# Attention values divided for all tiles at once, between two stages of a graph network kernel

## The reference

```
xm = x @ W_n2m;  e = edge_attr @ W_edge;  ee = e @ W_e
q, k, v = (xm @ W_q + b_q, xm @ W_k + b_k, xm @ W_v + b_v)   as (n, H=4, C=16)
alpha = sum(q[dst] * (k[src] + ee), -1) / sqrt(C)            one per edge and head
alpha = softmax of alpha over the edges with the same dst    = ex / den[dst]
out   = segment_sum((v[src] + ee) * alpha, dst)              (n, 64)
x_r   = xm @ W_skip + b_skip
beta  = sigmoid([out, x_r, out - x_r] @ W_beta)
x     = layernorm(x + (beta * x_r + (1 - beta) * out) @ W_m2n)
x     = layernorm(x + relu(x @ w1 + segment_sum((x @ w2)[src] * ew, dst) + b))
```

## Time and profile before

| | us |
|---|---|
| median of 3 timed executions | 1562.85 (1562.12 to 1571.67) |
| span of the one profiled execution, first to last instruction | 1705.3 |
| own time of that execution | not given beside its span |
| VectorE busy in it | 1346.5 (79%) |
| TensorE busy | 1245.0 (73%) |
| ScalarE busy | 1225.0 (72%) |
| GpSimd busy | 1042.2 (61%) |

### The profile page before, as it was taken

One profiled execution on the slowest core, in us unless ns is written; L12 is line 12 of the kernel. 1 busy time (PEld: TensorE's weight loads), 2 busy tenths in 40 slices (PEclk: granted clock), 3 DMA queues, 4 the chain that ended last, 5 costly groups with the idle time before them and its releaser, 6 DMA issues.

```text
span 1705.3 us, 34722 instructions
## 1 busy us (share of the span) xinstructions
PE 1245.0 (73%) x9184; PEld 1095.8 (64%) x9184; DVE 1346.5 (79%) x5156; ACT 1225.0 (72%) x4231; POOL 1042.2 (61%) x1182
## 2 busy tenths in 40 slices
PE   1888888888888882288877876788888876665661
PEld 1877777777777772177766766666666675554551
DVE  2777898889999998888877876799999984654653
ACT  0899999999999995077787876899999962222221
POOL 2666666555566660055555656888888846666665
PEclk9999999999999996599999997999999997787876
DMA  6899999999999996734444445899999942222221
GB/s 189 269 306 302 305 305 304 303 302 301 305 301 305 308 300 233 240 117 152 154 144 140 156 141 168 270 289 292 293 289 294 292 143 77 79 82 74 86 77 38
DMA packets 210148, 372.00 MB, mean 218 GB/s; under 512 B 36740, under 2 KB 67821, under 8 KB 208935
## 3 DMA queue, kind: packets, MB, share of 16 engines
q1 hardware_dynamic: 120822, 200.48, 37.2%
q10 hardware_dynamic: 57771, 108.12, 17.3%
q0 software_dynamic: 31360, 61.17, 13.2%
HBM read 231.39 MB, written 161.37 MB: 230 GB/s over the span
## 4 chain that ended last, share of the span: by engine, by line
ACT 36%; DVE 29%; issue 11%; another core or an unknown queue 9%; PE 9%; DMA 1%; POOL 1%; SPq 1%; DVEq 1%; ACTq 0%; POOLq 0%
ACT hout L728 10%; ACT scan_buf L728 10%; DVE stats L992 7%; DVE hpre L1238 6%; ACT big L756 4%; ACT em L688 3%; DVE big L1228 3%; DVE hpre L1314 2%; ACT lv L769 2%; PE pd L596 2%; DVE hout L1002 2%; DVE scan_buf L1002 2%; PE pd L597 2%; PE pk L619 2%
## 5 line engine op out<-in xcount | busy, mean ns | idle before, releaser
L992 DVE BATCH_NORM_STATS2 stats<-hpre 128x6 f32<-128x256 f32 x882 | 334.8, 421 | 1.8
L466 POOL DMA_INDIRECT ring_a<-in_x,gidx x196 | 185.6, 947 | 207.4 <-PE pt L556 146.7
L728 ACT ACTIVATE scan_buf<-hpre,nb,rs 128x128 f32<-128x128 f32 x686 | 292.1, 480 | 2.8 <-DVE scan_buf L1002 1.3
L728 ACT ACTIVATE hout<-hpre,nb,rs 128x128 f32<-128x128 f32 x686 | 292.2, 480 | 2.5 <-issue 1.2
L1098 DVE SCALAR_TENSOR_TENSOR hpre<-pd,beta,xg 128x128 f32<-128x128 f32 x784 | 221.3, 345 | 29.0 <-DVE beta L1091 1.0
L565 PE MATMUL pd<-w_sx,scan_buf 128*128 128x129 f32 x1568 | 229.7, 276 | 0.0
L469 POOL DMA_INDIRECT ring_b<-in_x,gidx x196 | 185.0, 944 | 60.0 <-issue 60.0
L619 PEld LDWEIGHTS pk<-w_sb,scan_buf 128*128 128x128 f32 x1568 | 211.5, 196 | 7.4
L499 POOL DMA_INDIRECT big<-h_tab,gidx x196 | 193.4, 987 | 35.0 <-POOL big L505 29.5
L619 PE MATMUL pk<-w_sb,scan_buf 128*128 128x128 f32 x1568 | 209.9, 278 | 0.0
L565 PEld LDWEIGHTS pd<-w_sx,scan_buf 128*128 128x128 f32 x1568 | 207.0, 192 | 2.7
(11 more groups left out here) (208 smaller groups left out, 3692.4 us busy)
## 6 DMA issues: line engine op xcount, KB each, us to landing
xg<-in_x SPq DMA_DIRECT2D x196, 256.0 KB
scan_buf<-in_xT SPq DMA_DIRECT2D x196, 256.0 KB
val<-h_tab SPq DMA_DIRECT2D x139, 256.0 KB
h_tab<-hout ACTq DMA_DIRECT2D x98, 256.0 KB
h_tab<-scan_buf ACTq DMA_DIRECT2D x98, 256.0 KB
out_z<-hout ACTq DMA_DIRECT2D x98, 256.0 KB
out_z<-scan_buf ACTq DMA_DIRECT2D x98, 256.0 KB
h_two<-h_tab SPq DMA_DIRECT2D x57, 256.0 KB, 9.1
```

What stands on the lines that cost most here:

```text
L466: gp.indirect_dma_start(out=ring_a[:, u, :], out_offset=None, in_=x[:, :], in_offset=bass.IndirectOffsetOnAxis(ap=gidx[:, k, 0:1], axis=0))\
L728: ins = act.activation(hout[ju][:, i * D:(i + 1) * D], hpre[:, ju, i * D:(i + 1) * D], ACT.Identity, bias=nb_of(ju, i), scale=rs_of(ju, i))
L992: ins = dve.bn_stats(stats[:, ju, i, :, :].rearrange("p j s -> p (j s)"), two)
```

## The change

The division moves out of b1. `val` is divided in place for all tiles, before b1. With a = 1 / denominator, the carried value (val + cexp * carn) * a is made as val * a + (cexp * a) * carn: VectorE first multiplies `cexp` by `alpha` (128x784), then `val` by `alpha`, one instruction of 128x3136 per head: VectorE does heads 0 and 1 (HD = 2), each ahead of the 16 carry additions of its head, and GpSimd heads 2 and 3, for whose ends VectorE waits on the new semaphore `scaled`. The gather `b1_gather_o`, its buffer and `os_b1` are gone. TensorE transposes the two tiles of a step straight from `val`, as two [128, 64] blocks whose elements lie 196 apart, each to [64, 128] beside the other in PSUM. ScalarE copies [64, 256] to one of four places, which lie in rows 0 to 63 or 64 to 127 of two buffers; the products read 64 rows of it and of `r_o`. SyncE's wait before it reuses `val` is on the last transpose, not on the last gather.

```diff
+    HD = 2
...
-        o3 = own[:, 2 * D:4 * D].rearrange("p (i n) -> p i n", i=2)
-        oT = [ring_b[:, 0, :], ring_b[:, 1, :], own[:, 4 * D:5 * D]]
+        o_two = [ring_b[:, 0:2, :].rearrange("p a f -> p (a f)"), own[:, 2 * D:4 * D]]
+        o_rows = val[:, :, :, :].rearrange("p h c t -> p (h c) t")
+        def oT(k):
+            return o_two[k // 2 % 2][k % 2 * DM:(k % 2 + 1) * DM, :]
...
+        def over_sum(eng, h):
+            return eng.tensor_tensor(val[:, h, :, :], val[:, h, :, :],
+                                     alpha[:, h, :].rearrange("p (a t) -> p a t", a=1).to_broadcast([P, C, T]), ALU.mult)
...  SyncE, load_h
                 if g == G1:
-                    sp.wait_ge(S["os_b1"], T2)
+                    sp.wait_ge(S["t_b1"], T2)
...  GpSimd, after the gathers of the first stage
+            gp.wait_ge(S["sc"], 6)
+            for h in range(HD, H):
+                over_sum(gp, h).then_inc(S["scaled"], 1)
...  TensorE
             def b1_turn(k):
-                pe.wait_ge(S["os_b1"], k + 1)
                 if k > 0:
                     pe.wait_ge(S["oT_b1"], k)
-                pe.transpose(pt[:, 1, 0:P], o3[:, k % 2, :], ident[:, :]).then_inc(S["t_b1"], 1)
+                for i in range(2):
+                    mm = pe.transpose(pt[0:DM, 1, i * P:(i + 1) * P], o_rows[:, :, 2 * k + i], ident[:, :])
+                mm.then_inc(S["t_b1"], 1)
...  b1_product
-                    mm = pe.matmul(pd_bank[:, j % 2, i, 0:D + 1], oT[j % 3], r_o[:, i, :], start=False, stop=True)
+                    mm = pe.matmul(pd_bank[:, j % 2, i, 0:D + 1], oT(j)[:, i * P:(i + 1) * P], r_o[j % 2 * DM:(j % 2 + 1) * DM, j % 2, :], start=False, stop=True)
...  ScalarE, b1_evict
-                if k > 2:
-                    act.wait_ge(S["mm_b1"], k - 2)
-                act.activation(oT[k % 3], pt[:, 1, 0:P], ACT.Copy).then_inc(S["oT_b1"], 1)
+                if k > 3:
+                    act.wait_ge(S["mm_b1"], k - 3)
+                act.activation(oT(k), pt[0:DM, 1, 0:2 * P], ACT.Copy).then_inc(S["oT_b1"], 1)
...  VectorE, between the stages
-            dve.reciprocal(alpha[:, :, :], alpha[:, :, :])
+            dve.reciprocal(alpha[:, :, :], alpha[:, :, :]).then_inc(S["sc"], 1)
+            dve.wait_ge(S["sc"], 6)
+            link(dve.tensor_tensor(cexp[:, :, :], cexp[:, :, :], alpha[:, :, :], ALU.mult))
             for h in range(H):
+                if h < HD:
+                    link(over_sum(dve, h))
+                else:
+                    dve.wait_ge(S["scaled"], h - HD + 1)
                 for c in range(C):
                     ins = dve.scalar_tensor_tensor(out=val[:, h, c, :], in0=cexp[:, h, :], ...)
...
-            def b1_gather_o(k):
-                if k > 1:
-                    dve.wait_ge(S["t_b1"], k - 1)
-                dve.tensor_tensor(o3[:, k % 2, :].rearrange("p (i h c) -> p h c i", i=2, h=H), ... )
...
-            for s in range(3):
-                b1_gather_o(s)
             for s in range(T2 + 2):
-                if s + 3 < T2:
-                    b1_gather_o(s + 3)
```

More of the change, by code:

```diff
@@ L246, in gnn_kernel @@
             "piece_a", "log_a", "sc", "sc_pe", "sc_act",
-            "os_b1", "t_b1", "oT_b1", "mm_b1", "cl_b1", "em_b1", "xb_b1", "ep_b1", "be_b1", "pre_b1", "bn_b1",
+            "scaled", "t_b1", "oT_b1", "mm_b1", "cl_b1", "em_b1", "xb_b1", "ep_b1", "be_b1", "pre_b1", "bn_b1",
             "lv_b1", "rs_b1", "h_b1", "na_b1",
@@ L579, in _ @@
             pe.transpose(pt[:, 1, 0:DM + H], cumT[0:DM + H, 0:P], ident[0:DM + H, 0:DM + H]).then_inc(S["sc_pe"], 1)
-            pe.wait_ge(S["sc"], 6)
+            pe.wait_ge(S["sc"], 7)
             def b1_turn(k):
-                pe.wait_ge(S["os_b1"], k + 1)
                 if k > 0:
                     pe.wait_ge(S["oT_b1"], k)
-                pe.transpose(pt[:, 1, 0:P], o3[:, k % 2, :], ident[:, :]).then_inc(S["t_b1"], 1)
+                for i in range(2):
+                    mm = pe.transpose(pt[0:DM, 1, i * P:(i + 1) * P], o_rows[:, :, 2 * k + i], ident[:, :])
+                mm.then_inc(S["t_b1"], 1)
             def b1_product(j):
@@ L637, in carry_turns @@
             def carry_turns():
-                pe.wait_ge(S["sc"], 7)
+                pe.wait_ge(S["sc"], 8)
                 pe.transpose(pt[:, 0, 0:P], sum_a, ident[:, :])
@@ L642, in carry_product @@
             def carry_product():
-                pe.wait_ge(S["sc"], 8)
+                pe.wait_ge(S["sc"], 9)
                 pe.matmul(pt[:, 1, 0:D], cumT[:, 0:P], w2_sb[:, :], start=True, stop=True).then_inc(S["sc_pe"], 1)
@@ L831, in d2_spread @@
                         S["bn_d2"], S["lv_d2"], S["rs_d2"], g)
-            act.wait_ge(S["sc"], 6)
+            act.wait_ge(S["sc"], 7)
             b1_evict(0)
@@ L1177, in _ @@
             ins.then_inc(S["sc"], 1)
-            dve.wait_ge(S["sc"], 6)
+            dve.wait_ge(S["sc"], 7)
             dve.tensor_tensor_scan(psame[:, :], same[:, :], same[:, :], 1.0, ALU.min, ALU.min)
-            def b1_gather_o(k):
-                if k > 1:
-                    dve.wait_ge(S["t_b1"], k - 1)
[L1185 to L1188, removed]
             def b1_mix(j):
```

## The result

The changed kernel takes 1620.9 us (1616.1 to 1627.8) where the kernel before takes 1562.5: a ratio of 1.0354 (95% interval 1.0307 to 1.0400), 58 us slower. The prediction was 1584 (1564 to 1598): the right side, and too little by 37 us.

A forecast was written before the change was run, and what follows sets the result against it. VectorE was taken to bound the serial stretch before b1 and, by a little, to pace b1. Serial piece +18.9 and loop +2 gave +21 us on the median 1562.85: 1584, range 1564 to 1598.

The forecast's parts named there:

- the stride: In b1, TensorE's transposes from `val` at 196 elements' stride: no price taken; even three times 0.11 us each leaves 5.9 a pair.
- TensorE's sum: In b1, TensorE's time for a pair of steps: 4.83 us plus 0.22 for the added transposes, 5.05.
- The sentence on what would prove it wrong: Signs against: VectorE's additions keep 0.333 us beside GpSimd, a pair clearly under 5.5 us, or transposes from `val` over 0.3 each.
- The serial piece: From the inversion to the first transpose: 8.0 - 0.9 + 11.8 = +18.9 us, between +6.6 and +27.6.
- scan and gather: Before the first transpose: the scan runs beside transposes (0.48 us) and the first gather goes (about 0.45), -0.9 us.
- the block: Before b1, GpSimd's two 3136-element instructions hold VectorE off 5.9 us each, 11.8 us in all; bounds 0 and 20.
- Rival 1: Before b1, GpSimd doesn't hold VectorE up: serial +7.1, loop +2, 1572 us; chance 0.20.
- rival 3: Before b1, GpSimd needs its full 10 us an instruction and holds VectorE throughout: +29, 1592 us; chance 0.12.
- The rest of the loop: In b1, the pace goes from VectorE's 5.70 us a pair to ScalarE's 5.74: +2 us, bounds -10 and +12.
- Rival 2: In b1, TensorE gets free of the gather's wait and all 42 us of it go: 1540 us; chance 0.08.
- Rival 4: In b1, ScalarE already paces, so the wider copy counts each step: 18.9 + 12 = +31, 1594 us; chance 0.10.
- The assumption about the unnamed waits: Some 153 us of waits on releasers the profile can't name, also in b1, were taken as hardly present in timed runs.

The follow-up runs named there:

- f2_full: The changed kernel with its products back at 128 rows, rows 64 to 127 zeroed by three memsets: 1581.7 us, 1.0147 times the kernel before.
- e0_before: The kernel before, unchanged, run again for a second profile, on a slow chip: 1738.6 us.

## Why the prediction was wrong

**The step that failed** is the sentence on TensorE in the loop: "The half-height products keep their columns, and so their time." It had no row behind it, for no product of the kernel before had 64 rows in b1, and unlike the stride, next to it in the same paragraph, it was given no bound. The columns did stay, but each going over to 64 rows and back cost 0.29 us, 1.16 us a pair, and the transpose behind it 0.05 more, 0.11 a pair. TensorE needed 5.05 + 1.16 + 0.11 = 6.32 us a pair by this, and 6.33 by the trace, and went past both engines ahead of it. The rest of TensorE's sum was exact: without the height the pair is 5.05 us. Among the rivals none had TensorE as the bound by its own work; the list looked for waits and for the two engines at the top, and took the 0.69 us between TensorE's 5.05 and ScalarE's 5.74 for safe. The sentence on what would prove it wrong named the transposes, the other new thing on that engine.

**The serial piece** was right in mechanism and nearly in size: forecast +18.9, measured +20.0. Its terms: 8.0 us of new work on VectorE (0.98 and twice 3.42, with the gaps 7.9); -0.9 for scan and gather (measured 20.0 - 7.9 - 12.9 = -0.8); the block 12.9 us, forecast 11.8 by scaling the 0.24 us of the earlier trace rows by the number of elements. The estimate from the Trainium skill (GPSIMD Engine Reference, § 3.1), 6.9 us an instruction and so 13.8 in all, was 0.9 too high, mine 1.1 too low. That scaling came so near partly by luck: it set the hold, and not GpSimd's working time, in proportion to the elements, and the working time was 6.6 us where the same scaling of 0.41 us gives 10. GpSimd's records took 7.6 and 10.0 us, not the forecast 6 to 7, since each holds its own wait for VectorE. Rival 1 (no hold) and rival 3 (10 us each) are excluded.

**The rest of the loop** was right. VectorE paced the kernel before at the forecast 5.70 us a pair. Without the height, ScalarE paces the changed one at 5.70 (forecast 5.74), and b1 comes out 0.7 us shorter, where +2 was forecast: f2_full, at 1581.7, is nearly the predicted 1584. Rival 2 (TensorE freed from the gather's wait, -42 us) is excluded by it: in f2_full TensorE has no such wait and b1 is the same. Rival 4 (ScalarE paced already, the wider copy counts in full, +12) too. The stride of 196 elements had no visible price: among 128-row products a transpose from `val` takes 0.11 us to the next start, as does one from the dense buffer.

**The assumption about the unnamed waits** held for the chips on which the change was timed. That was luck in part: it was a guess that the profiled execution alone had them, and in fact they come in timed runs too, on slow chips. On those they hide most of the loss (the changed kernel at 1.014 in place of 1.035).

**SyncE's wait** on the last transpose cost nothing, as forecast: the load of the ring in `val` was queued behind the last stores, 10 us after the last turn (1022.6 against 1012.2 us).

## What to carry to other kernels

Halving the height of a matmul did not shorten it here, and a 64-row one among 128-row ones costs a switch there and back: keep the zeros and the full height, or at least put the low ones side by side (one switch in place of two; its gain in total time was not measured where before takes 1561 us). When work is moved between engines, work out the third engine's time per round with each new form of instruction in it, and bound every form for which the profile has no row; the engine with the slack is where an unbounded term decides. An idle GpSimd is no free helper for two-input elementwise work while VectorE does the same: it took about twice as long (6.6 us against 3.42), and VectorE stood still meanwhile.

## What the runs showed of the hardware that I had not expected

- Going over from 128-row to 64-row matmuls and back costs 0.29 us each time, at a granted clock of 0.98 of full in b1, between products of 129 and 257 columns; a transpose right behind it takes 0.05 us more.
- GpSimd's TENSOR_TENSOR of 128x3136 keeps a two-input VectorE instruction waiting for 6.5 us as one block, and waits itself for VectorE's in the same way; the waiting is counted as busy time of whichever instruction comes next, so that a mean over the group (0.74 us for 16) hides it.
- A copy by ScalarE out of PSUM of 64 rows and 256 columns takes as long as one of 128 rows (0.36 us), and 0.375 us (median) from rows 0 to 63 to rows 64 to 127.
- The same program took 1561 to 1563 us (medians) in two sets of runs and 1710 to 1739 us in three others. On the slow ones ScalarE and VectorE went on late after TensorE's records: in b1 up to 4.7 us after the last record that they wait for (e0_before), with waits of up to 12.1 us in the last stage. The chips of the four sets of experiments were four, each used once, so whether it is the chip or something else of that time is open, and so is the cause.
